# Attention-pooled recommender on one core: the candidate load goes behind the second unit's history features, and the query products behind that unit's projection

## The chip, the cores and the metric

The kernel runs on one core of a Trainium2 chip. The metric is the device time of one execution in microseconds (us). TensorE (PE) does the matmuls, VectorE (DVE) masked sums and reductions, ScalarE (ACT) activations, GpSimd (POOL) masks and splits, and SyncE (SP) issues all loads. The engines run side by side and wait for each other through semaphores.

## The reference

For 512 users, with one candidate item and a history of 200 items each (128 features per item), the reference computes:

```
cand = candidate_features @ Wi + bi            # 512 x 64
hist = history_features @ Wi + bi              # 512 x 200 x 64
qh = cand @ Wq ; kh = hist @ Wk
scores = relu(qh[:, None, :] + kh) @ Wv        # 512 x 200, masked behind history_length
attn = softmax(scores)
interest = einsum('bs,bse->be', attn, hist)
avg = masked mean of hist over its items
x = concat([interest, cand, avg])
x = relu(bn(x @ W1 + b1)); x = relu(bn(x @ W2 + b2)); x = relu(bn(x @ W3 + b3))
return sigmoid(x @ Wo + bo)
```

## The kernel before

The users are split in two halves that lie in the upper and lower 64 partitions of most tiles. A *quad* is four users (two of each half), a *unit* is two quads, and there are 64 units. The features of a unit are one load of 800 KB (`load`, L191 to L196). There are six load slots, so units 1 to 5 are issued at once, and each later load waits until the unit that had its slot has been projected. All loads go through SP's one queue, in program order (L199 to L207): early parameters, first half of unit 0, lengths, second half of unit 0, candidates, units 1 to 5, late parameters, then the other units.

PE does for every unit, in program order:

- `project` twice (L386): history features by Wi into `hist_ps`, one quad per call. It waits for the unit's features and for the DVE sums that free its bank.
- from unit 1 on, `keys(unit - 1)` (L398): keys of the unit before into `key_ps`. It waits for the DVE sums of that unit and for the ReLUs of the unit before that, since `key_ps` holds one unit.
- `score` (L409) once in four units, and from unit 9 on `spread_attn` (L425) for two quads.

`queries` (L360 to L374) is called once, behind unit 0's projections. It makes the bias of the queries (L362, two products with one column, into `attn_ps`), the queries (L368, candidates by a folded weight, into `attn_ps`) and the candidates' embedding (L372, into `score_ps`). The last two read `candT`, the tile of the candidate load. ACT turns them into `query_bias`, `query` and `cand` (L331, L334, L336) and only then begins its ReLUs (L299), which add `query` as a bias: `relu(unit)` reads `key_ps` and writes `hidden`. DVE writes the masked history of each quad, `kept`, with its sum (L521). `warmup` matmuls (L358) and a product for the folded weight (L463) stand at PE's start. Nothing but the order of the code and the semaphores decides what runs when.

Of the kernel before, what the change touches and what calls it, by code (L numbers as in the profile page):

```python
# [53 lines left out]
def build(nc, hist_dram, cand_dram, params_dram, lens_dram, out_dram):  # L54
    with ExitStack() as ctx:
        def sb(name, shape, dt=F32):
            return ctx.enter_context(nc.sbuf_tensor(name, shape, dt))
# [4 lines left out]
        def sem(name):  # L62
            return ctx.enter_context(nc.semaphore(name))
# [12 lines left out]
        candT = sb("candT", [128, 2, QUADS, 2])  # L76
# [59 lines left out]
        cand_landed = sem("cand_landed")  # L136
# [48 lines left out]
        def wait(eng, semaphore, value):  # L185
            if value > 0:
                eng.wait_ge(semaphore, value)

        @block.sync
        def _(sp):  # L190
            def load(unit):  # L191

                wait(sp, hist_ready, 2 * (unit - LOAD_SLOTS + 1))
                slot = unit % LOAD_SLOTS
                sp.dma_start(history[:, slot, :, :, :].rearrange("f h p s -> f (h p s)"),
                             hist_dram[unit, :, :]).then_inc(batch_landed[slot], 16)  # L196

            hist_quads = hist_dram[0, :, :].rearrange("f (h p s) -> f h p s", h=2, p=4)
            sp.dma_start(params[:, 0:EARLY], params_dram[:, 0:EARLY]).then_inc(early_landed, 16)  # L199
            sp.dma_start(history[:, 0, :, 0:2, :], hist_quads[:, :, 0:2, :]).then_inc(first_quad_landed, 16)  # L200
            sp.dma_start(lens_raw[:, :], lens_dram).then_inc(lens_landed, 16)
            sp.dma_start(history[:, 0, :, 2:4, :], hist_quads[:, :, 2:4, :]).then_inc(batch_landed[0], 16)
            sp.dma_start(candT[:, :, :, :].rearrange("f u g h -> f (u g h)"), cand_dram).then_inc(cand_landed, 16)
            for unit in range(1, UNITS):
                load(unit)
                if unit == LOAD_SLOTS - 1:
                    sp.dma_start(params[:, EARLY:PARAMS], params_dram[:, EARLY:PARAMS]).then_inc(late_landed, 16)  # L207
            sp.wait_ge(result_ready, 2)
            sp.dma_start(out_dram.rearrange("(a n) -> a n", a=1), result[:, :, :].rearrange("a h n -> a (h n)")).then_inc(result_stored, 16)
            sp.wait_ge(result_stored, 16)  # L210
# [145 lines left out]
        def _(pe):  # L356
# [3 lines left out]
            def queries():  # L360
                for name in ("wk2", "wq2"):
                    product = pe.matmul(attn_ps[:, 1, 0:1], param(name, slice(0, EMB)), param("bi", slice(0, EMB)),  # L362
                                        start=(name == "wk2"), stop=(name == "wq2"))
                product.then_inc(bias_product, 1)
                pe.wait_ge(cand_landed, 16)
                pe.wait_ge(folded_ready, 1)
                for u in range(2):
                    product = pe.matmul(attn_ps[64 * u:64 * u + 64, 0, 0:HALF], folded[:, :],  # L368
                                        candT[:, u, :, :].rearrange("f g h -> f (g h)"), start=True, stop=True)
                product.then_inc(query_product, 1)  # L370
                for h in range(2):
                    product = pe.matmul(score_ps[64 * h:64 * h + 64, 0, 0:HALF], param("wi"),  # L372
                                        candT[:, :, :, h].rearrange("f u g -> f g u"), start=True, stop=True)
                product.then_inc(cand_product, 1)  # L374

            def project(g):
                unit, at = divmod(g, 2)
                slot = unit % LOAD_SLOTS
                if g == 0:
                    pe.wait_ge(first_quad_landed, 16)  # L380
                elif at == 0 or g == 1:
                    pe.wait_ge(batch_landed[slot], 16 * (unit // LOAD_SLOTS + 1))

                wait(pe, masked_summed, 2 * (g - 1))
                for h in range(2):
                    product = pe.matmul(hist_ps[64 * h:64 * h + 64, g % 2, 0:QCOLS], param("wi"),  # L386
                                        history[:, slot, h, 2 * at:2 * at + 2, :].rearrange("f p s -> f (p s)"),
                                        start=True, stop=True)
                product.then_inc(hist_ready, 1)

            def keys(unit):
                first = 2 * unit % KEPT_SLOTS
                pe.wait_ge(masked_summed, 4 * (unit + 1))

                wait(pe, relu_done, 4 * unit)
                for u in range(2):
                    for h in range(2):
                        product = pe.matmul(key_ps[64 * u:64 * u + 64, h, 0:QCOLS], key_weights(h),  # L398
                                            kept[64 * h:64 * h + 64, first:first + 2, u, :], start=True, stop=True)
                product.then_inc(key_ready, 1)  # L400

            def score(j):
                pe.wait_ge(relu_done, 2 * SB_QUADS * (j + 1))

                wait(pe, max_ready, j - 1)
                for k in range(4):
                    for c in range(4):
                        quad = (SB_QUADS * j + 2 * c + k % 2) % HID_SLOTS
                        product = pe.matmul(score_ps[32 * c:32 * c + 32, j % 2, 0:SEQ], wv_rows[:, k, :],  # L409
                                            hidden[:, quad, k // 2, :], start=(k == 0), stop=(k == 3))  # L410
                product.then_inc(scored, 1)

            def spread_attn(q):
                j, quad = divmod(q, SB_QUADS)
                if quad == 0:
                    pe.wait_ge(parts_ready, j + 1)

                if FREE_AT + 2 <= q < FREE_AT + 4:
                    pe.wait_ge(masked_summed, HALF)
                else:  # L420
                    wait(pe, attn_summed, 2 * (q - (4 if q >= FREE_AT + 4 else 2)) + 2)
                bank = attn_bank(q)
                for u in range(2):
                    for h in range(2):
                        product = pe.matmul(bank[64 * h:64 * h + 64, u * SEQ:(u + 1) * SEQ], spread[:, 2 * quad + u, h, :],  # L425
                                            parts[:, j % 2, :], start=True, stop=True)
                product.then_inc(attn_spread, 1)
# [38 lines left out]
            for unit in range(UNITS):  # L466
                project(2 * unit)
                project(2 * unit + 1)
                if unit == 0:
                    queries()  # L470
                if unit >= 1:
                    keys(unit - 1)
                j, at = divmod(unit - SCORE_AT, SB_UNITS)
                if at == 0 and j >= 0:
                    if j == 0:
                        pe.wait_ge(wv_ready, 1)
                        pe.wait_ge(cand_ready, 1)
                    score(j)
                if unit >= DELAY:
                    if unit == DELAY:  # L480
                        pe.wait_ge(spread_made, 1 + 2 * COPIES)
                        pe.wait_ge(query_ready, 1)
                    spread_attn(2 * (unit - DELAY))
                    spread_attn(2 * (unit - DELAY) + 1)
# [202 lines left out]
```

## Time and profile before

| | |
|---|---|
| median of 3 runs | 234.3 us (233.96 to 234.71) |
| profiled execution, its own time | 233.41 us |
| span of its trace | 231.3 us |
| PE busy | 214.4 us (93%) |
| DVE busy | 178.0 us (77%) |
| ACT busy | 103.8 us (45%) |
| POOL busy | 65.8 us (28%) |
| granted TensorE clock, mean | 0.979 |

The trace covers 231.3 us of the 233.41 us of its execution, so 2.1 us lie around it. Positions in the rows are us from the start of the span. Busy shares say which engine is loaded over the whole; what an edit at one place is worth is read at that place.

### The profile page before, as it was taken

To read this page: it belongs to the slowest core of one execution; us is meant where nothing else is said; L and a number is where in the kernel's file an instruction comes from. 1 tells how busy PE (TensorE), PEld (TensorE's weight loads), DVE (VectorE), ACT (ScalarE), POOL (GpSimd) and SP (SyncE) were. 2 spreads that over 40 slices of the span, in tenths; PEclk is the share of its full clock that TensorE was granted. 3 is DMA by queue.
4 is the path that set the end of the run, shared out by engine and by line. 5 is a ranking of instruction groups with operands and counts; after the bars stand their busy time and mean duration, and the time that the engine had idled before them with its cause. 6 is when DMAs were issued, how large, how long until landed. Compare 5 with 4: busy or idle time off the path is not lost.

```text
span 231.3 us, 6395 instructions
## 1 busy us (share of the span) xinstructions
PE 214.4 (93%) x2106; PEld 87.3 (38%) x2106; DVE 178.0 (77%) x1087; ACT 103.8 (45%) x302; POOL 65.8 (28%) x115
## 2 busy tenths in 40 slices
PE   5999989999999999999999999999999999975873
PEld 2423324343434343343434343434343344422431
DVE  0455556979797998979797979797988979799750
ACT  2035363545445354455353545454453554354123
POOL 6963060413223140505050403223140505040000
PEclk9999999999999999999999999999999999999587
DMA  6999997887868786868787987878687930000000
GB/s 175 376 423 417 420 348 267 281 284 252 292 220 287 248 294 249 291 221 300 233 290 255 292 278 243 301 238 298 224 291 257 294 137 3 0 4 0 3 0 2
DMA packets 10226, 53.72 MB, mean 232 GB/s; under 512 B 1105, under 2 KB 2001, under 8 KB 10194
## 3 DMA queue, kind: packets, MB, share of 16 engines
q1 hardware_dynamic: 10194, 53.32, 66.4%
q8 instruction: 17, 0.28, 0.6%
q14 instruction: 15, 0.12, 0.2%
HBM read 53.32 MB, written 0.00 MB: 230 GB/s over the span
## 4 chain that ended last, share of the span: by engine, by line
PE 77%; ACT 10%; issue 6%; DVE 4%; DMA 2%; SPq 0%; ACTq 0%; DVEq 0%
PE hist_ps L386 30%; PE key_ps L398 24%; PE score_ps L409 10%; PE attn_ps L425 9%; ACT hidden L299 6%; DMA history<-history_dram 2%; ACT weights L307 2%; DVE scratch L532 2%; PE key_ps L437 1%; DVE inv_len L592 1%; PE score_ps L448 1%; PE key_ps L443 1%; PE score_ps L456 1%; ACT x L315 0%; PE attn_ps L368 0%
## 5 line engine op out<-in xcount | busy, mean ns | idle before, releaser
L299 ACT ACTIVATE hidden<-key_ps,query 128x200 f32<-128x200 f32 x256 | 90.2, 428 | 101.0 <-PE key_ps L398 101.0
L521 DVE SCALAR_TENSOR_TENSOR kept<-item,lens,hist_ps 128x200 f32<-128x200 f32 x256 | 93.9, 419 | 14.1 <-PE hist_ps L386 14.1
L386 PE MATMUL hist_ps<-history,params 128*64 128x400 f32 x512 | 99.5, 510 | 1.4 <-DMA history<-history_dram 1.4
L532 DVE CUSTOM_DVE_ANT_0 scratch<-attn_ps,kept 128x200 f32<-128x200 f32 x248 | 76.1, 362 | 25.4 <-PE attn_ps L425 23.5
L398 PE MATMUL key_ps<-kept,params 64*64 64x400 f32 x512 | 57.9, 520 | 4.3 <-ACT hidden L299 3.7
L386 PEld LDWEIGHTS hist_ps<-history,params 128*64 128x64 f32 x512 | 32.8, 139 | 33.0 <-issue 30.1
L253 POOL TENSOR_SCALAR attn<-weights,inv_sum 128x200 f32<-128x200 f32 x15 | 6.5, 435 | 128.9 <-DVE inv_sum L548 128.9
L425 PE MATMUL attn_ps<-parts,spread 128*64 128x200 bf16 x496 | 34.9, 258 | 2.8 <-DVE attended L532 2.8
L425 PEld LDWEIGHTS attn_ps<-parts,spread 128*64 128x64 bf16 x496 | 19.7, 109 | 36.7 <-issue 30.7
L398 PEld LDWEIGHTS key_ps<-kept,params 64*64 64x64 f32 x512 | 14.1, 131 | 44.7 <-issue 37.6
L409 PE MATMUL score_ps<-hidden,wv_rows 128*32 128x200 f32 x512 | 25.0, 336 | 1.0 <-ACT hidden L299 1.0
L521 DVE DVE_READ_ACCUMULATOR kept<-item,lens,hist_ps 128x1 f32 x256 | 21.5, 84 | 0.0
L532 DVE DVE_READ_ACCUMULATOR2_ANT attended<- 128x1 f32 x256 | 21.4, 84 | 0.0
L409 PEld LDWEIGHTS score_ps<-hidden,wv_rows 128*32 128x32 f32 x512 | 15.0, 109 | 14.3 <-issue 9.4
L245 POOL TENSOR_SCALAR mask_bias<-item,lens 128x200 f32<-128x200 f32 x16 | 15.4, 961 | 1.5
L258 POOL TENSOR_TENSOR rest<-attn,part_a 128x200 f32<-128x200 f32 x15 | 8.5, 569 | 1.3
L265 POOL TENSOR_TENSOR parts<-rest,part_b 128x200 bf16<-128x200 f32 x15 | 8.5, 566 | 1.2
L307 ACT ACTIVATE weights<-scores,neg_max 128x200 f32<-128x200 f32 x16 | 7.4, 460 | 2.1 <-DVE neg_max L542 2.1
L255 POOL TENSOR_SCALAR part_a<-weights,inv_sum,params 128x200 bf16<-128x200 f32 x15 | 7.6, 507 | 0.0
L238 POOL TENSOR_SCALAR_AFFINE_SELECT spread<-spread 128x1024 bf16<-128x1024 bf16 x6 | 6.9, 1167 | 0.4
L260 POOL TENSOR_SCALAR part_b<-rest,params 128x200 bf16<-128x200 f32 x15 | 6.5, 435 | 1.5
L542 DVE CUSTOM_DVE_ANT_0 scores<-score_ps,mask_bias 128x200 f32<-128x200 f32 x16 | 5.8, 363 | 0.0
(67 smaller groups left out, 56.7 us busy)
## 6 DMA issues: line engine op xcount, KB each, us to landing
history<-history_dram SPq DMA_DIRECT2D x63, 800.0 KB, 4.7
history<-history_dram SPq DMA_DIRECT2D x2, 400.0 KB, 4.8
candT<-candidates_dram SPq DMA_DIRECT2D x1, 256.0 KB, 5.1
params<-parameters_dram SPq DMA_DIRECT2D x1, 248.5 KB, 12.3
params<-parameters_dram SPq DMA_DIRECT2D x1, 226.0 KB, 2.5
lens_raw<-lengths_dram SPq DMA_DIRECT2D x1, 136.0 KB, 4.4
probability<-result SPq DMA_DIRECT2D x1, 2.0 KB
```

The source lines that it names most:

```text
L245: pool.tensor_scalar(mask_bias[:, j % 2, :], item[:, :], row_len[:, j:j + 1], MASKED, ALU.is_ge, ALU.mult).then_inc(mask_ready, 1)
L255: pool.tensor_scalar(part_a[:, :], weights[:, bank, :], inv_sum[:, bank:bank + 1], param("keep1"), ALU.mult, ALU.mult).then_inc(split_step ...
L258: pool.tensor_tensor(rest[:, :], attn[:, :], part_a[:, :], ALU.subtract).then_inc(split_steps, 1)
L265: pool.tensor_tensor(parts[:, bank, :], rest[:, :], part_b[:, :], ALU.subtract).then_inc(parts_ready, 1)
L299: act.activation(hidden[:, g % HID_SLOTS, h, :], key_ps[:, h, at * SEQ:(at + 1) * SEQ], ACT.Relu, bias=query[:, 2 * g + h:2 * g + h + 1]). ...
L307: act.activation(weights[:, bank, :], scores[:, bank, :], ACT.Exp, bias=neg_max[:, bank:bank + 1], scale=-1.0, accum_out=weight_sum[:, ban ...
L386: product = pe.matmul(hist_ps[64 * h:64 * h + 64, g % 2, 0:QCOLS], param("wi"), history[:, slot, h, 2 * at:2 * at + 2, :].rearrange("f p s ...
L398: product = pe.matmul(key_ps[64 * u:64 * u + 64, h, 0:QCOLS], key_weights(h), kept[64 * h:64 * h + 64, first:first + 2, u, :], start=True, ...
L409: product = pe.matmul(score_ps[32 * c:32 * c + 32, j % 2, 0:SEQ], wv_rows[:, k, :], hidden[:, quad, k // 2, :], start=(k == 0), stop=(k == 3))
L425: product = pe.matmul(bank[64 * h:64 * h + 64, u * SEQ:(u + 1) * SEQ], spread[:, 2 * quad + u, h, :], parts[:, j % 2, :], start=True, stop ...
L521: dve.scalar_tensor_tensor(out=kept[:, g % KEPT_SLOTS, u, :], in0=item[:, :], scalar=pair_len[:, col:col + 1], in1=hist_ps[:, g % 2, u * S ...
L532: dve.tensor_tensor_reduce(scratch[:, q % 2, u, :], bank[:, u * SEQ:(u + 1) * SEQ], kept[:, q % KEPT_SLOTS, u, :], 1.0, 0.0, ALU.mult, ALU ...
```

## The change

Two statements move. On SP the candidate load is issued after the load of unit 1 instead of before it. On PE `queries()` is called behind the projections of unit 1 instead of behind those of unit 0. No other statement changes.

```
@@ -200,9 +200,10 @@
             sp.dma_start(history[:, 0, :, 0:2, :], hist_quads[:, :, 0:2, :]).then_inc(first_quad_landed, 16)
             sp.dma_start(lens_raw[:, :], lens_dram).then_inc(lens_landed, 16)
             sp.dma_start(history[:, 0, :, 2:4, :], hist_quads[:, :, 2:4, :]).then_inc(batch_landed[0], 16)
-            sp.dma_start(candT[:, :, :, :].rearrange("f u g h -> f (u g h)"), cand_dram).then_inc(cand_landed, 16)
             for unit in range(1, UNITS):
                 load(unit)
+                if unit == 1:
+                    sp.dma_start(candT[:, :, :, :].rearrange("f u g h -> f (u g h)"), cand_dram).then_inc(cand_landed, 16)
                 if unit == LOAD_SLOTS - 1:
                     sp.dma_start(params[:, EARLY:PARAMS], params_dram[:, EARLY:PARAMS]).then_inc(late_landed, 16)
             sp.wait_ge(result_ready, 2)
@@ -466,7 +467,7 @@
             for unit in range(UNITS):
                 project(2 * unit)
                 project(2 * unit + 1)
-                if unit == 0:
+                if unit == 1:
                     queries()
                 if unit >= 1:
                     keys(unit - 1)
```

On TensorE, from the first projection to the first keys, stands before (L386 projections, L362, L368 and L372 the three parts of `queries`, L398 keys):

```order
L386 MATMUL hist_ps<-history,params 64x400 [waits first_quad_landed]
L386 MATMUL hist_ps<-history,params 64x400
L386 MATMUL hist_ps<-history,params 64x400 [waits batch_landed0]
L386 MATMUL hist_ps<-history,params 64x400
L362 MATMUL attn_ps<-params 128x1 x2
L368 MATMUL attn_ps<-candT,folded 64x256 [waits folded_ready,cand_landed]
L368 MATMUL attn_ps<-candT,folded 64x256
L372 MATMUL score_ps<-candT,params 64x256 x2
L386 MATMUL hist_ps<-history,params 64x400 [waits masked_summed,batch_landed1]
L386 MATMUL hist_ps<-history,params 64x400
L386 MATMUL hist_ps<-history,params 64x400 [waits masked_summed]
L398 MATMUL key_ps<-kept,params 64x400 [waits masked_summed]
```

and now, at the same place on TensorE (every line number is higher by one):

```order
L387 MATMUL hist_ps<-history,params 64x400 [waits first_quad_landed]
L387 MATMUL hist_ps<-history,params 64x400
L387 MATMUL hist_ps<-history,params 64x400 [waits batch_landed0]
L387 MATMUL hist_ps<-history,params 64x400
L387 MATMUL hist_ps<-history,params 64x400 [waits masked_summed,batch_landed1]
L387 MATMUL hist_ps<-history,params 64x400
L387 MATMUL hist_ps<-history,params 64x400 [waits masked_summed]
L363 MATMUL attn_ps<-params 128x1 x2
L369 MATMUL attn_ps<-candT,folded 64x256 [waits folded_ready,cand_landed]
L369 MATMUL attn_ps<-candT,folded 64x256
L373 MATMUL score_ps<-candT,params 64x256 x2
L399 MATMUL key_ps<-kept,params 64x400 [waits masked_summed]
```

The six query products have moved past the four projections of unit 1, so the wait for unit 1's features (`batch_landed1`) now stands directly behind unit 0's projections. On SP, the queue from the lengths to the late parameters before:

```order
L201 DMA lens_raw<-lengths_dram 128x272
L202 DMA history<-history_dram 128x2x400
L203 DMA candT<-candidates_dram 128x512
L195 DMA history<-history_dram 128x1600 x5
L207 DMA params<-parameters_dram 128x497
```

and now:

```order
L201 DMA lens_raw<-lengths_dram 128x272
L202 DMA history<-history_dram 128x2x400
L195 DMA history<-history_dram 128x1600
L206 DMA candT<-candidates_dram 128x512
L195 DMA history<-history_dram 128x1600 x4
L208 DMA params<-parameters_dram 128x497
```

The candidates have moved behind one unit; units 2 to 5 and the late parameters have as much ahead of them as before.

## Rows read from the trace of the kernel before

**Rows 1.** Busy time by stretch: start and end, then each engine, clock, DMA, GB/s
```profile
9.10:10.00 0.90, 0.90 (x6) 0.89 (x4) 0.78 (x4) 0.00 (x0) 0.90 (x2) 1.00 1.06 427
10.00:11.70 1.70, 1.70 (x9) 1.00 (x10) 0.00 (x0) 0.65 (x2) 1.56 (x2) 1.00 1.00 418
...
38.00:186.00 148.00, 145.26 (x1540) 59.58 (x1536) 128.26 (x804) 71.54 (x217) 41.48 (x72) 1.00 0.79 267
```

**Rows 2.** Chain of waits, 0 to 30 us: start, length, what
```profile
5.94 3.19 PE hist_ps L386 x8
9.13 0.94 PE attn_ps L362 x4
10.07 1.05 PE attn_ps L368 x4
11.13 0.85 PE score_ps L372 x4
11.98 2.05 PE hist_ps L386 x8
14.03 0.83 PE key_ps L398 x8
...
19.01 0.90 PE key_ps L398 x8
19.91 1.49 PE hist_ps L386 x8
21.40 0.09 issue
21.49 0.90 PE key_ps L398 x8
```

**Rows 3.** Waits of PE from 60 to 200 us: total, times, longest
```profile
PE key_ps L398 <- ACT hidden L299: 2.5, 11, 0.2
```

**Rows 4.** Timeline, 0 to 40 us: start, busy, instructions [idle before]
```profile
5.94 3.19 PE L386 MATMUL hist_ps<-history,params 128*64 128x400 f32 x8 [1.36 <-DMA history<-history_dram]
7.53 0.30 PEld L386 LDWEIGHTS hist_ps<-history,params 128*64 128x64 f32 x4 [1.30 <-DMA history<-history_dram]
9.06 1.01 PE L362 MATMUL attn_ps<-params 64*128 64x1 f32 x4
10.00 1.12 PE L368 MATMUL attn_ps<-candT,folded 128*64 128x256 f32 x4
10.91 1.07 PE L372 MATMUL score_ps<-candT,params 128*64 128x256 f32 x4
11.77 2.26 PE L386 MATMUL hist_ps<-history,params 128*64 128x400 f32 x8
12.43 0.24 PEld L386 LDWEIGHTS hist_ps<-history,params 128*64 128x64 f32 x2 [0.43 <-issue]
13.10 0.23 PEld L386 LDWEIGHTS hist_ps<-history,params 128*64 128x64 f32 x2 [0.43 <-issue]
13.96 0.90 PE L398 MATMUL key_ps<-kept,params 64*64 64x400 f32 x8
14.79 1.56 PE L386 MATMUL hist_ps<-history,params 128*64 128x400 f32 x8
15.18 0.14 PEld L386 LDWEIGHTS hist_ps<-history,params 128*64 128x64 f32 x2 [0.19 <-issue]
15.52 0.14 PEld L386 LDWEIGHTS hist_ps<-history,params 128*64 128x64 f32 x2 [0.19 <-issue]
16.52 0.90 PE L398 MATMUL key_ps<-kept,params 64*64 64x400 f32 x8 [0.16 <-DVE kept L521]
```

**Rows 5.** DMA issues, whole trace and narrow windows: KB each, us to landing
```profile
candT<-candidates_dram SPq DMA_DIRECT2D x1, 256.0 KB, 5.1
...
history<-history_dram SPq DMA_DIRECT2D x1, 400.0 KB, 5.0
...
history<-history_dram SPq DMA_DIRECT2D x1, 800.0 KB, 7.0
...
history<-history_dram SPq DMA_DIRECT2D x1, 800.0 KB, 8.5
```

**Rows 6.** Timeline of SP's queue, 2 to 45 us
```profile
2.52 0.55 SPq L202 DMA_DIRECT2D history<-history_dram  x1
3.12 0.60 SPq L203 DMA_DIRECT2D candT<-candidates_dram  x1
3.76 3.18 SPq L195 DMA_DIRECT2D history<-history_dram  x5
```

**Rows 7.** Timeline, 0 to 40 us, ACT's first rows
```profile
11.17 0.47 ACT L334 ACTIVATE query<-attn_ps,query_bias 128x256 f32<-128x256 f32 x1 [0.89 <-PE attn_ps L368]
12.03 0.47 ACT L336 ACTIVATE cand<-score_ps,params 128x256 f32<-128x256 f32 x1 [0.38 <-PE score_ps L372]
14.99 1.38 ACT L299 ACTIVATE hidden<-key_ps,query 128x200 f32<-128x200 f32 x4 [2.49 <-PE key_ps L398]
```

**Rows 8.** L386 by durations (min/median/max ns): 5.8 to 13.2, then 14 to 18.5 us and its loads
```profile
L386 PE MATMUL hist_ps<-history,params x14: 591/874/929, 5.9 to 13.1; 128*64 128x400 f32 x14
...
L386 PE MATMUL hist_ps<-history,params x18: 499/499/550, 13.5 to 18.4; 128*64 128x400 f32 x18
L386 PEld LDWEIGHTS hist_ps<-history,params x16: 132/136/137, 14.8 to 18.1; 128*64 128x64 f32 x16
```

**Rows 9.** Waits of SP's queue, 12 to 200 us: total, times, longest
```profile
SPq L195 <- PE hist_ps L386: 155.2, 57, 4.6
```

**Rows 10.** Busy time by stretch, the tail, columns as in rows 1
```profile
211.25:214.67 3.42, 1.45 (x16) 0.56 (x16) 3.38 (x21) 1.53 (x3) 0.00 (x0) 1.00 0.00 0
214.67:218.09 3.42, 3.03 (x18) 2.10 (x20) 2.87 (x16) 0.00 (x0) 0.00 (x0) 0.50 0.02 5
218.09:221.50 3.41, 2.97 (x13) 0.84 (x12) 1.35 (x10) 0.75 (x1) 0.00 (x0) 0.50 0.00 0
```

More of the change, by code:

```diff
@@ L202, in _ @@
             sp.dma_start(history[:, 0, :, 2:4, :], hist_quads[:, :, 2:4, :]).then_inc(batch_landed[0], 16)
-            sp.dma_start(candT[:, :, :, :].rearrange("f u g h -> f (u g h)"), cand_dram).then_inc(cand_landed, 16)
             for unit in range(1, UNITS):
                 load(unit)
+                if unit == 1:
+                    sp.dma_start(candT[:, :, :, :].rearrange("f u g h -> f (u g h)"), cand_dram).then_inc(cand_landed, 16)
                 if unit == LOAD_SLOTS - 1:
@@ L468, in _ @@
                 project(2 * unit + 1)
-                if unit == 0:
+                if unit == 1:
                     queries()
```

## The prediction

> **What bounds the kernel now.** I read the page for the shares, then the busy time by stretch. From 38 to 186 us PE is busy 145.3 of 148 us, and DVE, the next, 128.3 [rows 1]. The waits say the same: after 60 us PE waits only for ACT's ReLUs, 2.5 us in all [rows 3]. The chain of waits runs through PE from its first projection on; in the early units each turn is keys 0.90, projections 1.49 and 0.09 of issue, 2.48 us [rows 2]. SP's later loads are all released by PE's projections [rows 9], so they follow PE and don't lead it. So PE's line has no slack that would swallow a late start: keys(0) starts at 13.96 [rows 4], and what moves this start should move the end by as much. That start is the number to work out.
>
> The timeline of the start is the place to read. PE projects unit 0 from 5.94 on, its second quad from 7.53, when that half lands (issued at 2.52 [rows 6], 5.0 us to landing [rows 5], so 7.52). The one-column products follow at 9.06, the queries at 10.00, the candidates' embedding at 10.91, unit 1's projections at 11.77, keys(0) at 13.96 [rows 4]. From 9.06 to 11.77 PE makes the six query products, and in that time unit 1's features land: issued at 3.76 [rows 6], 7.0 us to landing [rows 5], so 10.76. The queries hide the wait for unit 1, and unit 1 is there 1.0 us before PE asks for it.
>
> **TensorE's clock at the start.** All this runs at half speed. The granted clock is printed as 1.00 there [rows 1], but durations tell otherwise: weight loads of one shape take 0.23 us at 12.43 and 13.10 and 0.14 at 15.18 and 15.52 [rows 4], and projection matmuls have a median of 874 ns up to 13.1 and 499 ns from 13.5 on [rows 8]. So the level is 1.2 GHz until some 13.25 and 2.4 GHz after. A product of both halves takes 0.66 us at the low level (the loads at 12.43 and 13.10 are 0.67 apart) and 0.34 at the high one (15.18 to 15.52). Before it rose PE had worked from 9.06 without a gap.
>
> **The change part by part.** Nothing is added or removed, all is order.
>
> 1. The load of unit 1 no longer stands behind 256 KB of candidates. These landed at 3.12 + 5.1 = 8.22 [rows 5, 6], 0.70 us behind the load ahead of them (7.52). At the 418 GB/s of that stretch [rows 1] they are 0.63 us. Unit 1 therefore lands at 10.76 - 0.70 = 10.06. Bounds: 10.76 if nothing is gained, and 9.44 if its 800 KB moved at 427 GB/s [rows 1] from 7.52 on. The 10.06 takes a row as it is, so I keep it. SP's issue time (0.60 us for the candidates, 0.64 for a unit [rows 6]) costs nothing: the loads queue for 5 us and more after issue.
>
> 2. The candidates land where unit 1 landed, about 10.8 us. PE now asks for them near 13.9, so they have 3 us to spare. Units 2 to 5 and the late parameters have the same bytes ahead of them. Unit 2 lands at 4.40 + 8.5 = 12.9 [rows 5] (issued one of five steps of 0.64 behind unit 1 [rows 6]) and is asked for at 14.79 before, later now. Later loads wait for PE [rows 9], and those that unit 1 releases are released earlier, which buys nothing, since PE waits for no load there [rows 3].
>
> 3. PE is done with unit 0 a little before 9.06, and what is next in its order is the wait for unit 1. The query products that filled this time are behind it. PE stands until 10.06 + 0.04 (unit 0 landed at 5.90 by the chain and began at 5.94 [rows 2]) = 10.10, about 1.04 us. The wait for DVE's sums that stands there too was over (unit 1 began without a wait before, and the first sums need only unit 0).
>
> 4. Unit 1's projections are four products at 0.66, 2.65 us, done at 12.75. The one-column products began about 0.2 behind the end of the projections before (7.53 + 1.33 = 8.86, start 9.06), so they begin at 12.95. The queries are 2.71 us at the low level (9.06 to 11.77 [rows 4]). If the clock rises at 13.25 as before, 0.30 of this is done there and 2.41 are left, 1.2 at the high level: done at 14.45, and with the 0.1 that lay between projections and keys, keys(0) starts at 14.55. That is 0.6 later than 13.96. A shorter way to see it: 1.04 us idle at the low level is 0.52 us of work at the high level, since the same work is caught up after the rise. With the bounds of the landing the idle time is 0.4 to 1.75 us, the shift 0.2 to 0.9.
>
> 5. ACT: the query's 0.47 and the embedding's 0.47 [rows 7] came 2.5 us ahead of the first ReLU. The embedding's began 0.26 after PE had turned to its next product (11.77 to 12.03 [rows 4, 7]). Now PE turns to keys(0) at 14.55, so it runs from 14.8 to 15.3, and the first ReLU, 1.03 behind the start of keys(0) (13.96 to 14.99), is due at 15.6. keys(0) hides it with 0.3 us to spare; were keys(0) shorter by more than that, the rest would be added. DVE's sums for unit 1 are now done behind the queries instead of behind keys(0), but keys(1) at 16.52 waited for ACT's ReLUs (14.99 + 1.38 = 16.37 [rows 7]), so this gives nothing back.
>
> 6. The tail: the granted clock is 0.50, the 1.2 GHz level, from 214.67 to 221.50, after a stretch in which PE was busy 1.45 of 3.42 us [rows 10]. A start later by half a microsecond puts other products into it. PE was busy there 3.03 + 2.97 us; a tenth of this either way is 0.3. I take nothing and keep 0.3 for the range.
>
> The sum is +0.6 us on the profiled execution: 233.4 to 234.0. That execution lies 0.9 under the median of the runs shown, so on the median: 234.3 + 0.6 = 234.9 us, +0.26%. What a measurement of this kernel can tell from no change is about 0.3%, 0.7 us. The forecast is thus "no change that can be told", on its slow side.
>
> The Trainium skill ("TensorE: Matmul & The Clock Gate", the part on the clock gate) says that the low clock is the default, that sustained activity releases it, and that DMA waits between bursts of matmuls keep it low. It speaks against this change, which puts such a wait into the ramp. By it the rise could come later than 13.25; without it the sum above stands. The trace has a rise behind work without a gap and none behind the projections of unit 0, which have gaps before and between them, and doesn't say to which of the two 1 us of idle time belongs.
>
> **The rivals.**
>
> A. The clock rises later (slower). Place: the 1.04 us without work in front of unit 1's projections, and then the one-column products, which stream next to nothing, directly behind them. For it: the rise before came after work without a gap from 9.06, and in the tail the clock fell after a thin stretch [rows 10]. Against: projections are denser than the query products that they replace around 11 us. Price: if it rises only when the queries are done, these take 2.71 instead of 1.5 us (+1.2, with the 0.6: 236.1); if keys(0) is at the low level too, 1.66 instead of 0.83, +0.8 more (236.9). The middle is 236.5. Each microsecond that the rise slips costs half of one, so it decides from a slip of 0.2 us on, where 0.6 grows to 0.7.
>
> B. Unit 1 lands no sooner. A landing is that of a load's last part, and perhaps that part is not held up by the candidates. Then the idle time is 1.75 and the shift 0.9: 235.2, slower by 0.37%. Against it: landings came in order of issue, the candidates 0.70 behind their forerunner [rows 5, 6].
>
> C. The delay is swallowed, or the move does nothing that matters: 234.3. For it: ACT and PE turn at nearly the same pace in the early units, so that little may be lost in PE's line. Against: that turn is a loop that starts with keys(0), and starts later.
>
> D. Faster. Unit 1 lands at 9.44, and two units of dense projections so near each other let the clock rise earlier, say at 11.3. The two microseconds to 13.25 would go at twice the speed, a gain of 1.0, less 0.2 for the wait: 233.5. It needs both.
>
> **How the numbers follow.** Forecast, 0.6 with its bounds of 0.2 to 0.9: 0.52. A: 0.20. B: 0.08. C: 0.11. D: 0.09. The likeliest case gives 234.9. Runs of one kernel differ by 0.75 us, so a quarter of the forecast's chance (0.13) and most of B (0.07) are told as slower, with A 0.40; faster is most of D, 0.08; the rest, 0.52, is within 0.3%. The range goes from the low end of C with the spread (233.9) to most of A (236.6).
>
> **What would show it.** Right: PE idle for about 1 us from 8.9 on, ended by a DMA of the history; unit 1 landing near 10.1, candidates near 10.8 with nobody waiting; the query products behind the projections at 12.9; weight loads of 0.14 us from 13.3 on; keys(0) at 14.5 and all later units shifted by the same 0.6. Wrong: keys(0) before 14.0, or weight loads of 0.23 us still at keys(0) (A), landing at 10.7 (B), a shift that is gone by 60 us (C), no idle time in front of unit 1 (D).

## Result: slower by 1.1%, and the profile after

| | before | changed |
|---|---|---|
| median of 20 runs, side by side | 234.09 us (231.67 to 236.71) | 236.95 us (234.62 to 239.26) |
| profiled execution, its own time | 233.41 us | 237.08 us |
| span of its trace | 231.3 us | 234.9 us |
| mean granted TensorE clock | 0.979 | 0.958 |

The ratio of the times is 1.0108, with a 95% interval of 1.0079 to 1.0137. (It leaves out the longest executions, so it is a little under the ratio of the medians.) Forecast were 234.9 us and a range from 233.9 to 236.6.

The start, in the timeline of the changed kernel: start, busy, instructions, in brackets the idle time before them and what ended it.

```profile
5.52 1.60 PE L387 MATMUL hist_ps<-history,params 128*64 128x400 f32 x4 [0.94 <-DMA history<-history_dram]
8.62 1.60 PE L387 MATMUL hist_ps<-history,params 128*64 128x400 f32 x4 [1.50 <-DMA history<-history_dram]
10.56 2.93 PE L387 MATMUL hist_ps<-history,params 128*64 128x400 f32 x8 [0.34 <-DMA history<-history_dram]
13.43 0.79 PE L363 MATMUL attn_ps<-params 64*128 64x1 f32 x4
14.15 0.65 PE L369 MATMUL attn_ps<-candT,folded 128*64 128x256 f32 x4
14.63 0.82 PE L373 MATMUL score_ps<-candT,params 128*64 128x256 f32 x4
...
15.38 0.90 PE L399 MATMUL key_ps<-kept,params 64*64 64x400 f32 x8
15.50 0.47 ACT L337 ACTIVATE cand<-score_ps,params 128x256 f32<-128x256 f32 x1 [0.17 <-PE score_ps L373]
16.41 1.38 ACT L300 ACTIVATE hidden<-key_ps,query 128x200 f32<-128x200 f32 x4 [0.44 <-PE key_ps L399]
...
17.94 0.90 PE L399 MATMUL key_ps<-kept,params 64*64 64x400 f32 x8 [0.16 <-DVE kept L522]
```

PE stands three times for history features, 0.94 + 1.50 + 0.34 = 2.78 us, where before it stood 1.36 us once [rows 4]. keys(0) starts at 15.38 instead of 13.96, keys(1) at 17.94 instead of 16.52, both 1.42 later. The landings of the second half of unit 0 (issued at 2.52), of unit 1 (issued at 3.12) and of the candidates (issued at 3.76) are, in KB and us from issue:

```profile
history<-history_dram SPq DMA_DIRECT2D x1, 400.0 KB, 6.1
history<-history_dram SPq DMA_DIRECT2D x1, 800.0 KB, 7.4
...
candT<-candidates_dram SPq DMA_DIRECT2D x1, 256.0 KB, 7.4
```

So the half of unit 0 is there at 8.6 (7.5 before), unit 1 at 10.5 (10.76 before), the candidates at 11.2, 3 us before PE asks for them.

The tail, ACT's last rows of before: last exponent, the three layers' activations, the last sigmoid.

```profile
210.74 0.46 ACT L307 ACTIVATE weights<-scores,neg_max 128x200 f32<-128x200 f32 x1 [2.09 <-DVE neg_max L542]
...
219.06 0.75 ACT L315 ACTIVATE x<-key_ps,bn_shift,bn_scale 128x480 f32<-128x480 f32 x1 [6.25 <-PE key_ps L443]
221.71 0.75 ACT L319 ACTIVATE x<-score_ps,bn_shift,bn_scale 64x480 f32<-64x480 f32 x1 [1.90 <-PE score_ps L448]
223.54 0.74 ACT L323 ACTIVATE x<-score_ps,bn_shift,bn_scale 32x480 f32<-32x480 f32 x1 [1.08 <-PE score_ps L451]
...
229.49 0.28 ACT L327 ACTIVATE result<-score_ps,params 1x32 f32<-1x32 f32 x1 [0.44 <-PE score_ps L456]
```

And the same of the changed kernel.

```profile
212.17 0.46 ACT L308 ACTIVATE weights<-scores,neg_max 128x200 f32<-128x200 f32 x1 [2.09 <-DVE neg_max L543]
...
220.48 0.75 ACT L316 ACTIVATE x<-key_ps,bn_shift,bn_scale 128x480 f32<-128x480 f32 x1 [6.24 <-PE key_ps L444]
223.18 0.75 ACT L320 ACTIVATE x<-score_ps,bn_shift,bn_scale 64x480 f32<-64x480 f32 x1 [1.95 <-PE score_ps L449]
225.82 0.74 ACT L324 ACTIVATE x<-score_ps,bn_shift,bn_scale 32x480 f32<-32x480 f32 x1 [1.90 <-PE score_ps L452]
...
233.07 0.28 ACT L328 ACTIVATE result<-score_ps,params 1x32 f32<-1x32 f32 x1 [0.44 <-PE score_ps L457]
```

The last exponent is 1.43 us later and so is the first layer: 190 us of work carried the shift of the start unchanged. Then the third layer is 2.28 later and the last sigmoid 3.58. I call "tail" the time from the last exponent to the end of the span: 231.3 - 210.74 = 20.6 us before, 234.9 - 212.17 = 22.8 now. Why it grew stands in the granted clock. First before, then the changed kernel (columns as in [rows 1], the clock is the third from the end):

```profile
215.00:219.00 4.00, 3.94 (x22) 2.42 (x24) 3.23 (x20) 0.00 (x0) 0.00 (x0) 0.50 0.02 4
219.00:223.00 4.00, 3.06 (x16) 0.94 (x16) 1.77 (x11) 1.50 (x2) 0.00 (x0) 0.69 0.00 0
223.00:227.00 4.00, 2.19 (x28) 1.41 (x26) 2.16 (x15) 1.12 (x2) 0.00 (x0) 1.00 0.01 2
227.00:231.00 4.00, 1.53 (x8) 0.41 (x8) 0.00 (x0) 1.57 (x4) 0.00 (x0) 0.67 0.00 1
```

```profile
215.00:219.00 4.00, 3.05 (x20) 1.97 (x20) 3.42 (x19) 0.00 (x0) 0.00 (x0) 0.53 0.00 0
219.00:223.00 4.00, 3.56 (x19) 1.22 (x16) 1.87 (x12) 0.75 (x1) 0.00 (x0) 0.50 0.02 4
223.00:227.00 4.00, 3.83 (x22) 1.62 (x20) 1.93 (x13) 1.49 (x2) 0.00 (x0) 0.50 0.00 0
227.00:231.00 4.00, 2.93 (x16) 1.66 (x16) 1.34 (x9) 0.75 (x2) 0.00 (x0) 0.50 0.01 2
```

Both fall to the 1.2 GHz level near 215. Before it is back at 2.4 GHz for 223 to 227, in the changed kernel it stays low to the end. In this pair of traces the loss of 3.6 us is thus 1.4 at the start and 2.2 in the tail. The medians lie 2.9 apart, so the pair shows where time is lost, and not the average share of each place.

### The profile page after: what moved, and what is told of

Same layout as the page of the kernel before. It is cut to its first block, busy times and chain, and to the rows that moved or that the text cites. A ratio compares the mean times of both kernels' runs of the same rounds, so it can differ in the third digit from the quotient of the medians.

```text
span 234.9 us, 6395 instructions
## 1 busy us (share of the span) xinstructions
PE 217.8 (93%) x2106; PEld 88.1 (38%) x2106; DVE 177.4 (75%) x1087; ACT 103.8 (44%) x302; POOL 65.9 (28%) x115
## 4 chain that ended last, share of the span: by engine, by line
PE 75%; ACT 9%; issue 6%; DVE 4%; DMA 3%; SPq 1%; ACTq 0%; DVEq 0%
PE hist_ps L387 28%; PE key_ps L399 24%; PE score_ps L410 10%; PE attn_ps L426 9%; ACT hidden L300 6%; DMA history<-history_dram 3%; ACT weights L308 2%; DVE scratch L533 2%; PE score_ps L457 1%; PE key_ps L438 1%; PE score_ps L449 1%; PE score_ps L452 1%; PE key_ps L444 1%; DVE inv_len L593 1%; ACT x L316 0%
## 5 line engine op out<-in xcount | busy, mean ns | idle before, releaser
L426 PE MATMUL attn_ps<-parts,spread 128*64 128x200 bf16 x496 | 35.6, 260 | 2.8 <-DVE attended L533 2.8
L399 PEld LDWEIGHTS key_ps<-kept,params 64*64 64x64 f32 x512 | 14.1, 131 | 44.7 <-issue 38.2
L410 PEld LDWEIGHTS score_ps<-hidden,wv_rows 128*32 128x32 f32 x512 | 15.0, 109 | 14.3 <-issue 9.4
```

## Experiments

Unless another is named, each ratio is to the kernel before, timed on the same chip, with its 95% interval.

**The halves of the change.** `load_only` moves the candidate load and leaves `queries()` behind unit 0; `queries_only` is the other half.

```
load_only:     candidate load behind load(1);  if unit == 0: queries()
queries_only:  candidate load before load(1);  if unit == 1: queries()
```

> Only the candidate load moves behind unit 1; the queries stay behind unit 0's projections. Theory 1 (what follows a load in the queue slows its last part): unit 0's second half lands near 8.6 us instead of 7.5 as in the changed kernel, and the queries then wait for the candidates until about 11.2; keys(0) near 15.5 or later, total +1.5 to +3. Theory 2 (the late half was chance in that one execution): it lands near 7.5, the queries still wait for the candidates at 10.8, keys(0) near 14.9, +0.9.

> Only the queries move behind unit 1's projections; the loads keep the order of before. Theory 1: unit 0's second half lands at 7.5 as before, PE stands from 8.9 until unit 1 lands at 10.8, keys(0) near 14.9 (+0.9), and the runs lie as close together as those of before: +0.9 to +1.5 in all. Theory 2, the order on TensorE with its idle time is all that counts: the same as the changed kernel or worse, since unit 1 lands later: +2.5 to +3.

Measured: `load_only` 1.0064 (1.0032 to 1.0096), `queries_only` 1.0177 (1.0132 to 1.0222). In `load_only` the half of unit 0 landed early and PE then waited for the candidates:

```profile
7.26 0.89 PE L387 MATMUL hist_ps<-history,params 128*64 128x400 f32 x4 [1.20 <-DMA history<-history_dram]
8.08 0.60 PE L363 MATMUL attn_ps<-params 64*128 64x1 f32 x4
10.92 0.65 PE L369 MATMUL attn_ps<-candT,folded 128*64 128x256 f32 x4 [2.24 <-DMA candT<-candidates_dram]
...
14.97 0.90 PE L399 MATMUL key_ps<-kept,params 64*64 64x400 f32 x8
```

The half is there at 7.2 with the new load order, which speaks against theory 1 (large packets behind it hold it up). Theory 2 had this trace right (queries waiting to 10.9, keys(0) at 14.97), though its +0.9 us was too little: the ratio is worth +1.5. `queries_only` came out at +4.1 us, above what either theory said. Its trace has PE waiting for unit 1 until 10.60, keys(0) from 16.31 to 17.9 at the low level, and keys(1) at 19.94. The move of the queries does the harm; the move of the load, harmful alone, takes some of it back.

**What stands behind unit 0's second half.** `late_first` puts the late parameters, small packets too, where the candidates had been. `after_again` is the changed kernel again.

```
+            sp.dma_start(params[:, EARLY:PARAMS], ...).then_inc(late_landed, 16)
             for unit in range(1, UNITS):
                 load(unit)
                 if unit == 1:
                     sp.dma_start(candT..., cand_dram).then_inc(cand_landed, 16)
-                if unit == LOAD_SLOTS - 1:
-                    sp.dma_start(params[:, EARLY:PARAMS], ...).then_inc(late_landed, 16)
```

> The changed kernel with the late parameters (248 KB in packets of under 2 KB, about the size of the candidates) in the place that the candidates had, before unit 1. Theory 1 (big packets of unit 1 right behind unit 0's second half hold up its slowest part): that half lands at 7.5 again, unit 1 at 10.8; keys(0) near 14.9, total about +1 and with little spread. Theory 2 (chance, or the order on TensorE alone): as wide a spread as the changed kernel's, 234.6 to 239, and no earlier landing of the half.

> The changed kernel unaltered, for a second trace and a second set of times beside the others. Theory 1: unit 0's second half lands later than 7.9 us again, and the granted clock again stays at the low level to the end of the tail in many executions; median about +2.8. Theory 2 (chance): half landed by 7.6, keys(0) near 14.5.

Measured: `late_first` 1.0152 (1.0108 to 1.0195; 6 runs from 236.9 to 239.4), `after_again` 1.0120 (1.0074 to 1.0167). Theory 1 wanted `late_first` faster than the changed kernel, and it is not. And a trace with the old load order, of `before_tail_fill` below, has the half as late as the changed kernel had it:

```profile
8.39 1.60 PE L390 MATMUL hist_ps<-history,params 128*64 128x400 f32 x4 [2.09 <-DMA history<-history_dram]
9.92 1.01 PE L366 MATMUL attn_ps<-params 64*128 64x1 f32 x4
...
15.03 0.90 PE L402 MATMUL key_ps<-kept,params 64*64 64x400 f32 x8
```

Theory 1 falls as the explanation of a landing 1.1 us later: the landing of that half varies from one execution to the next in both orders. A small effect is not excluded. Over all 18 traces the half lands at 8.15 on average where unit 1 is issued right behind it, and at 7.85 where the candidates or the late parameters are, with ranges that overlap (7.2 to 8.6 and 7.5 to 8.5). The second trace of the changed kernel shows rival A in the flesh:

```profile
8.42 1.60 PE L387 MATMUL hist_ps<-history,params 128*64 128x400 f32 x4 [1.98 <-DMA history<-history_dram]
10.37 2.93 PE L387 MATMUL hist_ps<-history,params 128*64 128x400 f32 x8 [0.35 <-DMA history<-history_dram]
13.23 1.01 PE L363 MATMUL attn_ps<-params 64*128 64x1 f32 x4
14.17 1.12 PE L369 MATMUL attn_ps<-candT,folded 128*64 128x256 f32 x4
15.08 1.07 PE L373 MATMUL score_ps<-candT,params 128*64 128x256 f32 x4
16.08 1.61 PE L399 MATMUL key_ps<-kept,params 64*64 64x400 f32 x8
```

keys(0) takes 1.61 us instead of 0.90, so the low level lasted past 16, and keys(1) starts at 19.35, 2.8 later than before.

**Fills in the tail and at the start.** Two theories stand now: the loss is made at the start (idle time and a later rise), or by the clock in the tail. `before_tail_fill` and `after_tail_fill` add idle work for PE in the tail: 64x200 products on cleared data into a part of a bank that nobody reads.

```
+            def fill(n):
+                for _ in range(n):
+                    pe.matmul(score_ps[64:128, 0, 0:SEQ], warmup[:, 0:64], warmup[:, 0:SEQ], start=True, stop=True)
...
+            fill(2)    # behind each spread_attn and mlp_stage from score(LAST) on
```

`before_warm` adds four `keep_busy()` behind the folded weight's product (L463), `after_gap_fill` three behind each of unit 0's two projections.

> The kernel before with two extra 64x200 bf16 matmuls on warm-up data behind each spread and each stage of the last layers, from score of the last superblock on, so that PE is less idle in the tail. Clock theory: the granted clock stays at 2.4 GHz through the tail or falls later, and the time falls by 0.5 to 1.5 us against before, with less spread. Rival: the fills only stand in the way of the chain of the tail, +0.5 to +1.

> The changed kernel with the same fills in the tail. Clock theory: about 2 us of the loss are a tail at the low level (in its two traces the clock fell at 215 and 219 and did not rise again, in the trace before it was back at 221.5): the median falls by 1.5 to 2.5 us against the changed kernel, and what remains against before_tail_fill is the shift of the start alone, 1.4 to 2.8. Rival (the tail has nothing to do with the loss): it keeps its full distance of 2.7 from before_tail_fill, and its own median stays or rises.

> The kernel before with four more 128x400 warm-up matmuls behind the folded weight's product, where PE waits 1.4 us for the first history (they take 1.33 us at the low level). Clock theory: the rise comes nearer 7 to 10 us than 13.3, keys(0) near 13, the median 0.5 to 1 us under before. Rival: the rise stays at 13 and beyond, no change or +0.1.

> The changed kernel with three idle 128x400 matmuls of the warm-up kind behind each of unit 0's two projections, 1.0 us each time at the low level, where PE waits for the history anyway. Clock theory (half or more of the loss is a rise of TensorE's clock that comes later because PE stands idle): the rise is earlier, near 10 to 14 us instead of 13.9 to 17.9, keys(0) starts at 14 to 15, and the median falls by 1 to 1.5 us against the changed kernel, to about 235.4. Idle theory (only the missing work counts, the clock is not to be moved by it): no gain, or up to 0.5 us slower where the fill outlasts the wait.

Measured: `before_tail_fill` 0.9918 (0.9885 to 0.9952), `after_tail_fill` 0.9878 (0.9830 to 0.9925), `before_warm` 0.9891 (0.9841 to 0.9941), `after_gap_fill` 0.9966 (0.9930 to 1.0002), about 2 us under the changed kernel's mean. By the tail fill the changed kernel gained 4 us and the kernel before 1.5, and nothing of the difference between them was left; the expectation had kept 1.4 to 2.8 us of it for the start. The start can be moved too: in the trace of `before_warm` the clock is up at 3.8 and stays up, with keys(0) at 12.12, and in that of `after_gap_fill` it is up at 8.7, with keys(0) at 13.38. The trace of `before_tail_fill` has the clock at the high level through the tail (stretches first, then the last exponent in its timeline):

```profile
215.00:219.00 4.00, 3.37 (x37) 2.42 (x38) 3.90 (x22) 0.07 (x1) 0.00 (x0) 1.00 0.01 4
219.00:223.00 4.00, 3.23 (x36) 1.71 (x32) 2.22 (x16) 1.81 (x3) 0.00 (x0) 1.00 0.00 0
223.00:227.00 4.00, 3.28 (x36) 2.05 (x32) 2.04 (x13) 1.11 (x3) 0.00 (x0) 1.00 0.01 2
```

```profile
211.84 0.46 ACT L307 ACTIVATE weights<-scores,neg_max 128x200 f32<-128x200 f32 x1 [2.09 <-DVE neg_max L561]
```

Its tail is 230.6 - 211.84 = 18.8 us, though 46 products more stand in it. The fill does not always hold the clock: in four of the ten traces with a filled tail it was at the low level for one short stretch between 215 and 220 (the two of `after_both`, that of `before_both` and of `before_tail_fill3`), and the tails were 20.4 us. The six others are 18.8 us long, so with the same work in the tail the low stretch is worth 1.6 us.

**How much is the start?** The same two were run twice more, and two kernels with fills at both ends: `before_both` (tail and start) and `after_both` (tail, start and gaps; PE waits for a DMA behind the gap fills all the same, 0.27 to 0.79 us).

> before_tail_fill again, for a second trace and more times, beside the next kernel on the same chip. Median 232.3 to 233.3.

> after_tail_fill again. If the start of the changed kernel is later by what its traces show (keys(1) 1.4 to 2.8 us later than in the trace before), it is slower than before_tail_fill2 by 1 to 2 us: 233.8 to 234.8. If nearly all of the loss was the low clock in the tail, as the medians of the first pair (232.8 and 232.3) say, the two are within 0.7 us.

> The kernel before with the fills in the tail and the four matmuls behind the folded weight's product. If the clock costs at both ends and the costs add: 1.0 (start) + 1.7 (tail) under before, near 231.6, the best of all. If one undoes the other: 232.8.

> The changed kernel with the fills in the tail, the four matmuls at the start and three behind each projection of unit 0, so that TensorE has nearly no idle stretch before unit 1. If the changed order costs only its missing work once the clock is up early (1.0 us of wait at the high level less what both orders wait for unit 1): 0 to 1 us slower than before_both. If it costs nothing without the clock: within 0.5 us.

> The kernel before with the fills in the tail, a third set. With 24 runs so far its mean is 233.0: 232.6 to 233.5.

> The changed kernel with the fills in the tail, a third set; 18 runs so far have a mean of 233.2 against 233.0 of the same fills on before. Theory: the low clock in the tail is where the loss of the change shows, the start costs under 0.8 us on the average: within 0.8 us of before_tail_fill3. Rival: the traces are right for the average (keys(0) 1.6 us later) and the first sets were lucky: +1.2 or more. Its trace falls either into the kind with keys(0) near 16 or into one with keys(0) near 14, which must exist if the theory holds.

> before_both again (median 230.4, but of 6 runs from 229.0 to 234.7). If the costs of the clock at both ends add, a mean of 230.5 to 231.5 and the fastest of all; keys(0) near 12 to 13 in its trace.

> after_both again (mean 232.0, of 6 runs). With both ends filled the changed order has only its missing work at the start: 0.3 to 1.2 us slower than before_both2.

The ratios: `before_tail_fill` 0.9941 and 0.9949, `after_tail_fill` 0.9957 and 0.9925 (each about 0.004 either way); `before_both` 0.9805 (0.9743 to 0.9868) and 0.9816 (0.9775 to 0.9858); `after_both` 0.9888 (0.9833 to 0.9942) and 0.9862 (0.9822 to 0.9903). The filled pairs kept within the 0.7 and 0.8 us expected of a loss in the tail, and `before_both` gained about 1 us more than the two costs of its expectation add up to. Put together, as means of all executions, the interval of each difference by drawing the runs anew:

| pair (runs) | changed order | old order | difference, us |
|---|---|---|---|
| no fill (26, 86) | 237.0 | 234.6 | +2.4 (1.9 to 2.9) |
| tail filled (30, 36) | 233.1 | 233.1 | 0.0 (-0.5 to +0.5) |
| tail and start filled (12, 12) | 231.8 | 230.5 | +1.3 (0.2 to 2.2) |

The rows of this table take all runs of a kernel over several sessions, so they say less than the side-by-side ratios on the last tenths. By the ratios the changed order lies -0.9, +0.4 and -0.6 us behind the old one with the tail filled, and +1.9 and +1.1 with both ends filled. With the tail filled the changed order costs nothing that these times can tell. Its start is not always as early, though. Two of its three traces with filled tail have keys(0) at 16, the third at 14.3, and there the rise came while unit 1's projections ran:

```profile
10.02 2.63 PE L391 MATMUL hist_ps<-history,params 128*64 128x400 f32 x8 [0.56 <-DMA history<-history_dram]
12.57 0.60 PE L367 MATMUL attn_ps<-params 64*128 64x1 f32 x4
...
14.34 0.90 PE L403 MATMUL key_ps<-kept,params 64*64 64x400 f32 x8
```

The one-column products take 0.60 us there and 1.01 in the trace before. The three traces of the old order with filled tail have keys(0) at 15.0, 14.5 and 14.6. So the start of the changed order is at times a little earlier and at times much later than the old one's.

The late kind is best seen where the clock rises once during the warm-up matmuls and falls again. The stretches from 14 to 18 us, `before_tail_fill` first, then `after_again`:

```profile
14.00:16.00 2.00, 2.00 (x16) 0.54 (x14) 1.55 (x8) 0.00 (x0) 1.51 (x3) 0.86 1.06 442
16.00:18.00 2.00, 1.84 (x16) 0.59 (x15) 1.19 (x7) 1.38 (x4) 0.00 (x0) 1.00 0.97 395
```

```profile
14.00:16.00 2.00, 2.00 (x10) 0.93 (x9) 0.12 (x2) 0.65 (x2) 1.57 (x3) 0.50 1.00 416
16.00:18.00 2.00, 2.00 (x12) 0.60 (x12) 0.00 (x0) 0.66 (x2) 0.00 (x0) 0.53 1.00 404
```

In the three such traces of the old order (the three of `before_tail_fill`) the clock is back up at 14.1 to 14.9 and keys(1) starts at 17.0 to 17.6. In the four with the queries moved (`after_again`, `late_first`, two of `after_tail_fill`) it is back at 17.6 to 18.2, and keys(1) starts at 19.3 to 19.4, 2 us later.

So the 0.0 of the filled pair does not say that the start is free, for the fill does not hold the clock equally in both orders: of the three traces each, one of the old order has the low stretch in its tail and none of the changed order. The traces without a start fill (four of the old order, five of the changed) have keys(1) at 17.1 and 18.6 on average, 1.5 apart, and scatter by 0.5 and 1.1. What the start costs on the average thus stays open between 0 and about 1.5 us. With the start filled too, +1.3 is left; the interval is wide, and in both traces of `after_both` but only one of two of `before_both` the tail has the low stretch, so this is not the start's cost alone either.

The trace of `before_both2` is the fastest start:

```profile
7.62 0.89 PE L390 MATMUL hist_ps<-history,params 128*64 128x400 f32 x4 [0.60 <-DMA history<-history_dram]
8.45 0.60 PE L366 MATMUL attn_ps<-params 64*128 64x1 f32 x4
...
11.84 0.90 PE L402 MATMUL key_ps<-kept,params 64*64 64x400 f32 x8
```

keys(0) at 11.84, 2.1 us before the kernel before. `before_both` is the version that beats both kernels: the old order with 4 products more at the start and 46 at the end, 2% under before.

## Why the prediction was wrong

The direction was right as far as it went (0.26% slower, called no change), the size was not: +0.6 forecast, +2.9 between the medians. Two terms of the sum failed, the tail (step 6) most and the start's clock (step 4) next.

- **Step 6, the tail, failed.** "I take nothing and keep 0.3 for the range." The tail was 2.2 us longer in the trace (20.6 to 22.8), since the granted clock did not come back. The unfilled and the filled pairs, +2.4 and 0.0, show that the loss is gone when the tail is filled; as the fill leaves the two orders with unlike tails, they don't show that all of it was made there. I had the row with the 0.50 in hand [rows 10], and priced a small shift against it, as if the clock's two changes stayed where they were and only the work moved. The filled tails show that the clock answers to the work. The price should have been the tail at the low level throughout: PE's products there are twice as long (the third layer's two 1.80 instead of 0.99 us), and each is waited for.
- **Step 1**: unit 1 landed at 10.5, not 10.06; 0.25 us sooner than before instead of 0.70. Over all 18 traces unit 1 landed at 10.3 on average where it is issued right behind unit 0 and at 10.6 where the candidates or the late parameters stand between, so the move gains 0.3 us on average and not the 0.70 taken. The bound of 10.76 held in the changed kernel (10.0 to 10.5).
- **Step 2** held: candidates at 11.2, asked for at 14.15; no later unit was waited for.
- **Step 3**: 1.42 us more idle time instead of 1.04, most of it in front of unit 0's second half, which landed 1.1 later. The order need not be the cause: `before_tail_fill` has it as late.
- **Step 4, the start's clock, failed too**: the rise was taken as fixed at 13.25. The two traces of the changed kernel have it at 13.9 and 17.9, and `queries_only` at 19.1. keys(0) at 15.38 and 16.08 lies behind the 14.55 of the sum, so the shift was 1.4 and 2.1 us instead of 0.6. Not every start is so late (14.34 in one filled run), and the average is open, as said above.
- **Step 5** held: the embedding's activation ended at 15.97, the first ReLU began at 16.41.
- **PE has no slack** held to the hundredth: 1.42 at keys(0), 1.43 at the last exponent.
- **The spread** was taken as 0.75 us from three runs; 20 runs of the kernel before span 5.0 us.

Rival A had the right agent but only one of its two places. It happens at the start (`after_again`): with the old order on TensorE and no fill there the traces have the rise at 13.3 to 14.9, with the queries moved at 12.2 to 19.1. That the clock also decides the tail no rival said. B, C and D did not decide; a piece of D is real, a rise at 12.2, during unit 1's projections.

What stays open: why the old order finds the clock back in its tail more often. The mean granted clock of an execution was 0.975 or more in 22 of 86 executions before and in none of 26 of the changed kernel. That mean also takes in low stretches at the start, so it doesn't count tails, and it is not the whole of the loss: the 64 other executions before took 234.8 us on average, still 2.2 less than the changed kernel.

The traces tie the tail to the moment at which the clock falls, more than to the order. Without a tail fill there are eight:

| clock falls, us behind the last exponent | traces | after it | tail, us |
|---|---|---|---|
| 2.9 to 3.3 | `after`, `queries_only`, `after_gap_fill`, `before_warm` | low to the end | 22.8 |
| 3.9, 4.5 | `before`, `load_only` | back at the high level | 20.6 |
| 5.4, 5.7 | `late_first`, `after_again` | low to the end | 21.9 |

`before_warm` has the old order and the long tail (last exponent at 208.8, end at 231.6). A start that shifts the tail against the clock's changes would thus change which tail a kernel gets. That is argued from eight traces, not shown; no run here moved the tail alone by a known amount.

## What to carry to other kernels

This kernel, with an idle TensorE at either end, paid by the clock for what happened there, and a shift of one microsecond at the start may change which tail it gets. Before pricing a shift, look whether the granted clock changes in the tail, and price both levels, not the mean. Idle matmuls on cleared data, put where TensorE waits, are cheap to try, and it helps to compare two orders of work with them in place: they take away much of the part of a difference that is only the clock's, though not all of it, so look at the clock in the filled traces too.

## What the runs showed of the hardware

- The start's low level is not in the granted clock: the stretches before the first change print 1.00 while weight loads of one shape take 0.23 us instead of 0.14. In traces where the clock rose once during the warm-up matmuls and fell again, it is printed as 0.50 from about 8 to 14 or 18 us.
- 46 extra products in the tail made it 1.8 us shorter (20.6 to 18.8) in the traces in which the clock stayed up. The Trainium skill ("TensorE: Matmul & The Clock Gate", Part 1) says that idle time sends the clock back to the low level and that activity releases it. The filled tails agree in direction, but no long gap was needed here: in the kernel before the clock fell at 214.67, and from 200 us to there PE's longest idle gap was 1.01 us.
- One 400 KB load, issued at 2.52 in each trace, was ready for PE between 7.26 and 8.62 us in the traces without a fill at the start. In every trace half of its 16 parts were there by 6.9, so it is the last parts that vary.
